# Row maxima of attention scores: one VectorE operation per pair of PSUM banks, and two banks for probability scores

## The reference

```
q = (x @ W_UQ).reshape(b, t, h, hd)
scores = jnp.einsum('bqhd,bkhd->bhqk', q, k) * scale
scores = jnp.where(causal, scores, -inf)
probs = jax.nn.softmax(scores, axis=-1)
ctx = jnp.einsum('bhqk,bkhd->bqhd', probs, v)
```

## Time and profile before

| what | before |
|---|---|
| median of three runs | 1242.43 us |
| runs | 1249.1, 1240.59, 1242.43 us |
| span of the profiled execution | 1240.9 us |
| mean granted TensorE clock, share of 2.4 GHz | 0.899 |
| PE busy, share of the span | 1069.9 us, 86% |
| DVE busy | 787.0 us, 63% |
| ACT busy | 491.9 us, 40% |
| POOL busy | 390.4 us, 31% |

### The profile page before, as it was taken

How to read it: one execution, slowest core, us unless ns; L and a number is a source line. 1 busy time by engine, 2 the same in 40 slices (tenths; PEclk the granted TensorE clock), 3 DMA queues, 4 the chain that set the end, 5 groups by cost and what they waited for, 6 DMA issues and landing times. The chain is left out here.

```text
span 1240.9 us, 19607 instructions
## 1 busy us (share of the span) xinstructions
PE 1069.9 (86%) x5364; PEld 554.3 (45%) x5365; DVE 787.0 (63%) x2352; ACT 491.9 (40%) x1043; POOL 390.4 (31%) x721
## 2 busy tenths in 40 slices
PE   6897599999999999998587553089999999999995
PEld 2443123333333333332176543046666666666663
DVE  5654599999999999894057443245555555555553
ACT  2333047777777777777501212012122122122121
POOL 2224513333333333333403235512222222222222
PEclk9878569999999999999987565589999999999998
DMA  2665974444466644400266641212232232232232
GB/s 91 208 189 188 199 157 104 122 113 113 116 141 135 132 82 79 80 20 30 66 220 193 225 124 68 103 39 44 46 50 42 45 49 42 44 49 42 44 49 25
DMA packets 102396, 121.22 MB, mean 98 GB/s; under 512 B 26352, under 2 KB 81776, under 8 KB 102320
## 3 DMA queue, kind: packets, MB, share of 16 engines
q1 hardware_dynamic: 89024, 102.55, 32.5%
q0 software_dynamic: 13296, 17.77, 8.6%
HBM read 70.27 MB, written 49.63 MB: 97 GB/s over the span
## 5 line engine op out<-in xcount | busy, mean ns | idle before, releaser
L640 ACT ACTIVATE b_prob<-b_prob_ps 128x512 f32<-128x512 f32 (+3 forms) x768 | 318.0, 506 | 103.2 <-PE b_prob_ps L684 101.2
L596 DVE CUSTOM_DVE_ANT_0 b_max_ps<-b_max_ps,b_mask_max 128x384 f32<-128x384 f32 (+3 forms) x512 | 246.7, 503 | 50.4 <-PE b_max_ps L666 47.9
L666 PE MATMUL b_max_ps<-b_k_st,b_q_st 96*128 96x512 bf16 (+3 forms) x768 | 253.5, 345 | 24.2 <-DMA b_k_st<-k_parts 21.8
L684 PE MATMUL b_prob_ps<-b_q_st,b_k_st 99*128 99x512 bf16 (+3 forms) x768 | 239.5, 330 | 10.5 <-ACT b_prob L640 6.6
L554 POOL TENSOR_SCALAR_AFFINE_SELECT b_prob<-b_prob 128x128 f32<-128x128 f32 x512 | 146.6, 292 | 308.6 <-ACT b_prob L640 300.9
L1352 POOL DMA_INDIRECT out_dram<-e_y,e_token x71 | 110.1, 1551 | 326.1 <-DVE e_y L1406 310.4
L599 DVE TENSOR_REDUCE b_neg_max<-b_max_ps 128x1 f32<-128x512 f32 x256 | 176.1, 688 | 5.1 <-PE b_max_ps L666 2.6
L666 PEld LDWEIGHTS b_max_ps<-b_k_st,b_q_st 96*128 96x128 bf16 x768 | 74.4, 99 | 202.0 <-DVE b_neg_max L596 110.1
L703 PE MATMUL b_acc_ps<-b_prob,b_v_aug 128*32 128x512 f32 (+3 forms) x1536 | 163.4, 498 | 0.2 <-POOL b_prob L554 0.2
L1459 PE MATMUL e_g_ps<-w_sb,e_rowsT 128*128 x284 | 135.5, 600 | 0.3 <-issue 0.3
L1459 PE MATMUL e_a_ps<-w_sb,e_rowsT 128*128 x284 | 134.0, 594 | 0.0
(11 more groups left out here) (164 smaller groups left out, 1093.4 us busy)
## 6 DMA issues: line engine op xcount, KB each, us to landing
w_sb<-in_L_ffn_W SPq DMA_DIRECT2D x11, 1024.0 KB, 11.3
e_rows<-slot_rows SPq DMA_DIRECT2D x72, 129.0 KB, 2.1
ctx_cols<-b_ctx_out SPq DMA_DIRECT2D x16, 512.0 KB
q_parts<-a_part_q SPq DMA_DIRECT2D x8, 768.0 KB, 3.8
k_parts<-a_part_k SPq DMA_DIRECT2D x8, 768.0 KB, 4.2
b_q_st<-q_parts SPq DMA_DIRECT2D x16, 384.0 KB, 5.0
b_k_st<-k_parts SPq DMA_DIRECT2D x16, 384.0 KB, 7.7
a_x<-in_L_attn_x SPq DMA_DIRECT2D x8, 512.0 KB, 6.5
```

The source lines that it names most:

```text
L596: nc.vector.tensor_tensor_reduce(scores, scores, mask_max[:, HALF - width:HALF], -1.0, -MASKED, ALU.add, ALU.min, to).then_inc(max_done, 1)
L640: nc.scalar.activation(prob[n % NP][:, 0:width], prob_ps[n % NS][:, 0:width], ACT.Exp, scale=SCALE).then_inc(prob_ok, 1)
L666: nc.tensor.matmul(out[:, 0:width], q_st[g % RING][0:STACK, h, i * P:(i + 1) * P], k_st[g % RING][0:STACK, h, half * HALF:half * HALF + wi ...
L684: nc.tensor.matmul(prob_ps[n % NS][:, 0:width], k_st[g % RING][0:MAXROWS, h, j * P:(j + 1) * P], q_st[g % RING][0:MAXROWS, h, q0:q0 + widt ...
```

## The change

One slot for maxima is now two banks (1024 columns); there are two such slots (NM = 2) in place of three single banks, and probability scores have two banks (NS = 2) in place of three: 4 + 2 + 2 banks. Two consecutive maxima matmuls write the two halves of a slot; only the first of them waits for the slot, and VectorE's count `max_done` now counts slots ("pairs"). `MAX_BLOCKS` is put in another order, so that in three of the six pairs of blocks both halves belong to the same query tile, and one `tensor_tensor_reduce` of 768, 1024, 640 or 896 columns reduces them together. (In the other three pairs the two halves are different tiles, and two operations are needed.) All reductions are now `tensor_tensor_reduce`, the mask is bf16 and 1024 columns wide, and the step that combined the halves' maxima falls away.

```diff
-MAX_BLOCKS = [(2, 0), (3, 0), (1, 0), (4, 0), (0, 0), (5, 0), (6, 1), (6, 0), (5, 1), (7, 0), (4, 1), (7, 1)]
+MAX_BLOCKS = [(3, 0), (0, 0), (5, 0), (5, 1), (7, 0), (7, 1), (2, 0), (1, 0), (4, 0), (4, 1), (6, 0), (6, 1)]
...
-    NM, NS = 3, 3
+    NM, NS = 2, 2
...
-    COMBINE_STEPS = 5
+    COMBINE_STEPS = 4
...
-            max_items += [("score", unit * QUAD + h) for h in range(QUAD)]
+            max_items += [("pair", unit * QUAD // 2 + h) for h in range(QUAD // 2)]
...
-        mask_max = sb("b_mask_max", [P, HALF])
+        mask_max = sb("b_mask_max", [P, SEQ], BF16)
...
-        max_ps = several(ps, NM, "b_max_ps", [P, HALF])
+        max_ps = several(ps, NM, "b_max_ps", [P, SEQ])
...
-            for unit in range(TOTAL):
...
-                    if diagonal:
-
-                        nc.vector.tensor_tensor_reduce(scores, scores, mask_max[:, HALF - width:HALF],
-                                                       -1.0, -MASKED, ALU.add, ALU.min, to).then_inc(max_done, 1)
-                    else:
-                        nc.vector.tensor_reduce(to, scores, AX.X, ALU.max, negate=True).then_inc(max_done, 1)
...
+            def reduce(n, i, half, width):
+
+                dve.wait_ge(max_sc_ok, n + 1)
+                g, h = n // PER_QUAD, block_at(n)[1]
+                at = half * HALF
+                scores = max_ps[place["pair", n // 2] % NM][:, at:at + width]
+                return nc.vector.tensor_tensor_reduce(scores, scores, mask_max[:, SEQ - width:SEQ], -1.0, -MASKED,
+                                                      ALU.add, ALU.min, neg_max[g % 2][:, h, i:i + 1])
+
+            for n in range(0, TOTAL * QUAD, 2):
+                g, u = divmod(block_at(n)[0], UNITS)
+                i, _, width = max_unit(u)
+                i_next, half_next, width_next = max_unit(u + 1)
+                if i == i_next:
+                    reduce(n + 1, i, 0, width + width_next).then_inc(max_done, 1)
+                else:
+                    reduce(n, i, 0, width)
+                    reduce(n + 1, i_next, 1, width_next).then_inc(max_done, 1)
...
-                bank_free(item)
-                out = max_ps[place[item] % NM]
-                nc.tensor.matmul(out[:, 0:width], q_st[g % RING][0:STACK, h, i * P:(i + 1) * P],
+                if n % 2 == 0:
+                    bank_free(item)
+                out = max_ps[place[item] % NM][:, n % 2 * HALF:n % 2 * HALF + width]
+                nc.tensor.matmul(out, q_st[g % RING][0:STACK, h, i * P:(i + 1) * P],
```

More of the change, by code:

```diff
@@ L367, in max_unit @@
     i, half = MAX_BLOCKS[u]
-    width = min(HALF, (i + 1) * P - half * HALF)
-    return i, half, width, i < (half + 1) * PER_HALF
+    return i, half, min(HALF, (i + 1) * P - half * HALF)
 def block_at(k):
@@ L399, in attention_phase @@
     PER_QUAD = UNITS * QUAD
+    PAIRS_PER_QUAD = PER_QUAD // 2
     HT = QUAD * QT
@@ L560, in combine @@
             def combine(g, step):
[L562 to L564 removed]
+                whole = neg_max[g % 2][:].rearrange("p h t -> p (h t)")
                 if step == 0:
[L567 to L569 removed]
@@ L570, in combine @@
                     if g >= 1:
                         dve.wait_ge(rows_ps_ok, g)
-                    dve.wait_ge(chain, 4 * g + 1)
+                    dve.wait_ge(max_done, (g + 1) * PAIRS_PER_QUAD)
                     nc.vector.tensor_copy(max_part[:, 0, :], whole).then_inc(chain, 1)
+                elif step == 1:
+                    dve.wait_ge(chain, 3 * g + 1)
+                    nc.vector.tensor_tensor(max_rest[:], whole, max_part[:, 0, :], ALU.subtract).then_inc(chain, 1)
                 elif step == 2:
-                    dve.wait_ge(chain, 4 * g + 2)
@@ L577, in combine @@
-                    nc.vector.tensor_tensor(max_rest[:], whole, max_part[:, 0, :], ALU.subtract).then_inc(chain, 1)
+                    dve.wait_ge(chain, 3 * g + 2)
+                    nc.vector.tensor_copy(max_part[:, 1, :], max_rest[:]).then_inc(chain, 1)
                 elif step == 3:
[L579 to L582, removed]
+                    dve.wait_ge(chain, 3 * g + 3)
@@ new lines, in _ @@
+            for n in range(0, TOTAL * QUAD, 2):
[7 more added lines that the diff above has]
+                    reduce(n + 1, i_next, 1, width_next).then_inc(max_done, 1)
+                if g >= 1 and n // 2 - g * PAIRS_PER_QUAD < COMBINE_STEPS:
+                    combine(g - 1, n // 2 - g * PAIRS_PER_QUAD)
@@ L650, in bank_free @@
                 kind, n = max_items[place[item] - NM]
-                if kind == "score":
+                if kind == "pair":
                     pe.wait_ge(max_done, n + 1)
@@ L658, in max_scores @@
                 g, u = divmod(unit, UNITS)
-                i, half, width, _ = max_unit(u)
-                item = ("score", n)
+                i, half, width = max_unit(u)
+                item = ("pair", n // 2)
                 if u == 0 and h == 0:
                     pe.wait_ge(stack_ok[g % RING], 16 * LOADS * (g // RING + 1))
-                bank_free(item)
-                out = max_ps[place[item] % NM]
-                nc.tensor.matmul(out[:, 0:width], q_st[g % RING][0:STACK, h, i * P:(i + 1) * P],
+                if n % 2 == 0:
+                    bank_free(item)
+                out = max_ps[place[item] % NM][:, n % 2 * HALF:n % 2 * HALF + width]
+                nc.tensor.matmul(out, q_st[g % RING][0:STACK, h, i * P:(i + 1) * P],
                                  k_st[g % RING][0:STACK, h, half * HALF:half * HALF + width],
```

13 lines of the change are left out of this document (2 added, 11 removed).

## The result

| what | before | after |
|---|---|---|
| median (runs) | 1243.18 us (4) | 1315.32 us (4) |
| lowest to highest | 1240.59 to 1249.1 | 1313.33 to 1320.05 |
| span of the profiled execution | 1240.9 us | 1313.9 us |
| mean granted TensorE clock | 0.899 | 0.903 |
| VectorE busy | 787.0 us | 779.5 us |

The changed kernel is slower by the ratio 1.0594 (95% interval 1.0548 to 1.064; the two medians by themselves give 1.058). The forecast was 1310 us, 1288 to 1326.

The account below looks back on a forecast made before the run. TensorE's program, with the probability bank's 1.07 us loop in it, was taken as the bound. 64.7 + 4.8 - 1.6 = +67.9 us on the 1240.9 us span gives 1308.8; the runs' median adds 1.5: 1310 us, range 1288 to 1326.

Parts of the forecast that it names:

- What bounds the kernel: TensorE's program sets the pace, including a probability bank's 1.07 us loop of matmul, exponential and release; three banks just cover it.
- about 0.9 with P0. The rest is a wait: In u3, TensorE's work makes about 0.9 of the 1.07 us from P0 to P3; the rest waits for ScalarE's exponential.
- Two banks: In the middle, P2 instead of P3 meets the 1.07 us loop: +4.41 us a quad, +64.7 us in all.
- a copy: In u0 and u6 an accumulator copy ahead of P0's exponential adds about 0.15 us each, bounds none and 0.35.
- P3's wait for P1's exponential: In the widest units it ends 1.45 to 1.55 us after P0, P3 comes at 1.46 to 1.51: nothing added.
- The wait that goes: P0's two waits for the maxima's DMA shrink: -1.6 us, bounds 0 and -1.6.
- The last stretch: The last 16 units, probabilities without maxima, each lose 0.22 to 0.47 us, 0.3 taken: +4.8 us.
- The rival of a falling clock: Stalls in every unit drop TensorE to 1.2 GHz: about 250 us more than forecast, about 1560 us; chance 0.03.
- Wide operations: A masked reduction of 1024 columns takes 1.12 us (1.10 to 1.24); VectorE's 2 us a quad gain counts 0.
- Two slots: M0 and M2 waiting for two-bank slots costs 0 while P2 waits; uncovered, up to 0.3 us in four units.
- Maxima alone: First 16 units: fewer operations against slots needing two slow-clock matmuls, taken as 0, between -2.6 and +3 us.
- The sum of 67.9: Total added time in us: 64.7 from two probability banks, 4.8 in the last units, less 1.6 of DMA waits.

Follow-up runs that it names:

- `b_ns2`: The kernel before with two probability banks in place of three, nothing else changed: 1313.03 us, ratio 1.0575.
- `a_two_ops`: The changed kernel, slots and block order kept, but each bank reduced by its own operation with the combining step back: 1317.54 us, ratio 1.0618.
- the filled kernel: The changed kernel with two more 512-column matmuls, results unread, ahead of P2 in 13 of the last units: 1307.91 us, ratio 1.0593.
- the repeat: The changed kernel run once more without any edit: 1312.45 us, ratio 1.0598.
- `a_ns3`: The changed kernel with three probability banks; products write one accumulator bank without accumulating, accumulator copies read a constant: 1267.37 us, ratio 1.0208.
- `a_short_exp`: The changed kernel with every exponential cut to at most 256 columns: 1274.06 us, ratio 1.0247.
- `b_v_early`: The kernel before with the products moved from the end of a unit to between P2 and M3: 1255.85 us, ratio 1.0155.
- `b_p3_late`: The kernel before with only P3 moved behind the products: 1227.89 us, ratio 0.9897.
- `a_ns3_narrow`: The changed kernel with three probability banks, one accumulator bank, constant-reading copies, and the narrow block first in each pair: 1253.82 us, ratio 1.0135.

## Why the prediction was right, and where its sizes were off

**What bounds the kernel: right, with one wrong sentence.** TensorE's program is the bound, and the third bank just covers the loop; `b_ns2` shows it, since without that bank every unit grows. But the prediction's "about 0.9 with P0. The rest is a wait" was a bad sum. P0, M1, P1, M2, P2 and M3 of u3 make 0.22 + 0.22 + 0.06 + 0.12 + 0.22 + 0.22 = 1.06, and P0 to P3 in the earlier trace rows is 1.07: TensorE hardly waited there. The 0.23 of the earlier trace rows is the weight load's idle time, not TensorE's. The same mistake the prediction had warned of, a load's wait read as a stall, was made a paragraph later. It did no harm, because the sum used the measured 1.07 and the pieces start to start.

**Two banks: right in size.** A quad was forecast at 31.84 and measured at 31.84; u4 at 2.98 and u5 at 2.34, measured 3.00 and 2.36. P0 to P2 is 1.07 in ten units of twelve and 1.21 in u0 and u6, so a copy adds 0.14 where 0.15 was taken. That the sum agrees to the hundredth is luck: over the quad of the rows above, M0 to P0 measures 2.60 where 2.54 was added, P2 to P3 4.18 for 4.14 and P3 to the products 2.43 for 2.52, and these cancel. Two sums of the prediction are slightly off: its pieces for u4 make 2.99, not 2.98, and the terms of its own range reach 1327, not 1325. P3's wait for P1's exponential, called a tie, adds nothing that can be seen in the sum. The middle grew by 64.0 against 64.7 - 1.6 = 63.1. Most of that 0.9 is the clock's rise at the beginning of the middle, at 178.3 and not 174.1: u4 and u5 of that quad lose some 0.6 us more against their usual length than they did before. In `a_two_ops`, where the clock rose at 173.1, the middle is 1.0 shorter than in the changed kernel.

**The wait that goes: right.** Quads that had waited for the maxima's DMA take 31.84 like the others.

**The last stretch: 4.8 forecast, 8.2 measured.** The 0.3 a unit was right: 8.2 less the 3.4 for the clock is 4.8, and the filled kernel shows 4.5. The step that failed is "the clock at 1.00 from the first probabilities on". The rival of a falling clock was set aside because the last stretch of before kept 1.00 with a wait in each unit, and the new units of the middle are denser. That holds for the middle. But the last stretch itself gets sparser too, and the prediction compared the middle with it and never the stretch with itself. The clock fell there in all four profiles of unfilled kernels with two banks and whole exponentials: for 10.3 us after the change, 10.2 in `b_ns2`, 3.4 in the repeat and in three spells, 34 us in all, in `a_two_ops`. It did not fall before, in `a_ns3`, `a_short_exp`, `b_v_early` and `b_p3_late`, or filled. `a_ns3_narrow` had a spell of 3.4 us with three banks, so it isn't the bank count alone, and what makes it fall stays open. The Trainium skill, TensorE: Matmul & The Clock Gate, "A second HAM failure mode: psum-queue depth-cycling", which the prediction had priced for the middle, tells of a clock that swings between its levels in a kernel that cycles through PSUM banks. The trace agrees with that in the last stretch (0.89 as its mean clock) and not in the middle (1.00), which cycles through the same two banks; that the cycling is the cause no run here shows.

**Wide operations: right.** 1024 columns take 1.15 to 1.18, between the bounds 1.10 and 1.24; the 1.12 taken was a little low. Their gain lay under TensorE's time, as `a_two_ops` shows with the same quad.

**Two slots: right while covered.** The forecast put their price at "0 while P2 waits" and up to 0.3 without that cover; `b_ns2` against the changed kernel gives the 0, and `a_short_exp` the other side: P2 1.18 after P0 in u6 and 0.97 in u0, 0.33 and 0.12 past its loop, in two units where four were allowed for.

**Maxima alone: 0 forecast, +0.7 measured**, inside its bounds and with its reason: a slot wants both banks filled before VectorE may start. The sum of 67.9 falls 5.1 short of the span's 73.0, but for rounding: 3.4 for the clock, 0.9 in the middle, 0.7 here and 1.1 by which attention began later, less the 0.9 after it.

## What to carry to other kernels

Before PSUM banks are moved from one use to another, add up the round trip of a bank (here matmul to exponential 0.42, exponential 0.60, release 0.05) and lay it beside the work that TensorE has between two uses of that bank: the rotation needs as many banks as make the second at least as long as the first. In u3 that work is 0.62 us between two uses with two banks and 1.06 with three, against a round trip of 1.07. The Trainium skill, Perfetto Trace Analysis, "Matmuls", gives the principle, to rotate independent matmuls through different banks so that emptying one overlaps the next; these runs add that going from just enough to one too few cost 4.4 us of 27.4 in each quad. Fewer operations on an engine that wasn't last brought nothing here, so the banks that they need were paid for in full; and a matmul that waits can be put behind work that nobody waits for (`b_p3_late`), but not together with one whose result the next unit needs (`b_v_early`).

## What the runs showed of the hardware that was not expected

The granted clock of TensorE can fall from 1.00 to 0.50 in the middle of a stretch in which it is busy three quarters of the time (12.64 of 17.10 us) and come back 10.3 us later, with the same kind of work before and behind. In the one profile with two extra matmuls a unit it stayed at 1.00, and the stretch took 41.5 us in place of 45.2 and 42.8. How long the spell lasts differs from run to run (10.3 and 3.4 us for the same kernel), so single profiles of such a stretch differ by some microseconds, and one without a spell doesn't show what prevents it.

VectorE needs 1.15 to 1.18 us for a masked reduction over two banks where two of one bank take 0.62 each. The Trainium skill, VectorE: DVE Perf Modes, section on the TRN2 errata, says of SBUF latency that one large tile pays it once and many small ones each. The prediction put this as access latency at large; these operations read the mask from SBUF but the scores from PSUM, and the trace shows a saving in the same direction. What a run here adds is that in the stretch where VectorE is busiest the first quad was still longer, 23.93 against 23.20 us, since the wide one starts later.
